# Expert weights of a mixture-of-experts layer: all resident in SBUF and selected by a register on TensorE, instead of one load for each tile

## What is computed

```python
h = patches(x) @ W.T + b                                  # 768 -> 192
h = h + attention(layernorm(h))                           # 12 heads, softmax of scores minus 0.2 x their 8 neighbours
x = layernorm(h)
score = relu(x @ Wr1.T + br1) @ Wr2.T + br2
mask = top_k(score, K); w = softmax(where(mask, score, -inf))
for e in range(E):
    mid = relu(x @ W1[e].T + b1[e]); ye = mid @ W2[e].T + b2[e]
    out = out + w[..., e:e + 1] * ye
h = h + out
```

## Time and profile before

| what | us |
|---|---|
| median of 3 runs | 2078.61 (2074.81 to 2085.45) |
| the profiled execution: span of its instructions | 2041.0 |
| expert phase in it | from 1144.7 |
| first matmul of tile 0 | 1206.69 |
| PE busy | 1849.8 (91% of the span) |
| DVE / ACT / POOL busy | 1458.3 / 1287.1 / 1139.5 |
| `wst` loads | 56 of 1584 KB, median 8.3 to landing |
| HBM read / written | 223.20 MB / 125.83 MB |

### The profile page before, as it was taken

How to read it: one execution, slowest core, us unless ns; L and a number is a source line. 1 busy time by engine, 2 the same in 40 slices (tenths; PEclk the granted TensorE clock), 3 DMA queues, 4 the chain that set the end, 5 groups by cost and what they waited for, 6 DMA issues and landing times. The chain is left out here.

```text
span 2041.0 us, 54475 instructions
## 1 busy us (share of the span) xinstructions
PE 1849.8 (91%) x18013; PEld 1378.2 (68%) x18013; DVE 1458.3 (71%) x4506; ACT 1287.1 (63%) x2661; POOL 1139.5 (56%) x1070
## 2 busy tenths in 40 slices
PE   4898998899889989898898579999999999999996
PEld 4666766666666666666665457777777777767774
DVE  4798889888988898889887456565665655574442
ACT  4688888888888888888888334444444444433332
POOL 4345464645555555555552356766767667664444
PEclk8898999999999999999998569999999999999998
DMA  4586665656566565656554358887888889878985
GB/s 154 147 253 195 186 203 166 196 181 192 174 191 189 179 185 180 194 185 192 174 173 120 102 175 194 197 211 192 199 216 195 198 206 197 198 188 182 187 183 83
DMA packets 362520, 373.10 MB, mean 183 GB/s; under 512 B 144516, under 2 KB 326080, under 8 KB 358272
## 3 DMA queue, kind: packets, MB, share of 16 engines
q1 hardware_dynamic: 320704, 329.03, 55.3%
q0 software_dynamic: 41664, 42.12, 12.3%
HBM read 223.20 MB, written 125.83 MB: 171 GB/s over the span
## 5 line engine op out<-in xcount | busy, mean ns | idle before, releaser
L2021 ACT ACTIVATE mh<-mid_bank 128x512 bf16<-128x512 f32 x336 | 200.6, 597 | 415.2 <-PE mid_bank L1622 415.2
L1923 DVE SCALAR_TENSOR_TENSOR ml<-mid_bank,mh 128x512 bf16<-128x512 f32 x336 | 232.0, 690 | 320.0 <-ACT mh L2021 319.3
L874 DVE TENSOR_REDUCE row_max<-s_bank 98x2 f32<-98x392 f32 x768 | 394.2, 554 | 53.6 <-PE s_bank L650 51.6
L1072 ACT ACTIVATE probs<-t_bank 98x392 f32<-98x392 f32 x768 | 339.7, 499 | 103.9 <-PE t_bank L666 100.5
L2097 POOL DMA_INDIRECT out_rows<-y_out,tail x168 | 267.4, 1592 | 160.7 <-DVE y_out L1957 114.1
L1636 PE MATMUL y_bank<-wst,mh 128*128 128x192 bf16 x1344 | 330.7, 246 | 0.8 <-DVE y_out L1957 0.8
L1639 PE MATMUL y_bank<-wst,ml 128*128 128x192 bf16 x1344 | 330.7, 246 | 0.0
L1638 PE MATMUL y_bank<-wst,mh 128*128 128x192 bf16 x1344 | 330.5, 246 | 0.0
L650 PE MATMUL s_bank<-k_stack,q_stack 96*98 96x196 f16 x1536 | 234.6, 259 | 46.2 <-DVE row_max L874 32.9
L1248 POOL TENSOR_TENSOR x_lo<-x_buf,x_hi 128x588 f16<-128x588 f32 x128 | 170.5, 1344 | 175.1 <-DVE x_b L939 73.0
L666 PE MATMUL t_bank<-q_stack,k_stack 104*98 104x196 f16 x1536 | 225.3, 259 | 32.8 <-ACT probs L1072 29.6
(11 more groups left out here) (257 smaller groups left out, 4527.6 us busy)
## 6 DMA issues: line engine op xcount, KB each, us to landing
wst<-packed SPq DMA_DIRECT2D x56, 1584.0 KB, 8.3
x_buf<-in_x_t SPq DMA_DIRECT2D x32, 1176.0 KB, 7.9
q_stack<-stack_parts SPq DMA_DIRECT2D x288, 98.0 KB, 2.5
k_stack<-stack_parts SPq DMA_DIRECT2D x288, 98.0 KB, 2.6
stack_parts<-qk_hi SPq DMA_DIRECT2D x32, 588.0 KB, 2.9
stack_parts<-qk_lo SPq DMA_DIRECT2D x32, 588.0 KB, 3.1
out_rows<-h_buf SPq DMA_DIRECT2D x32, 294.0 KB
h_in<-out_rows SPq DMA_DIRECT2D x32, 294.0 KB
```

The source lines that it names most:

```text
L874: nc.vector.reduce_max(row_max[st.odd][:, :, hh:hh + 1], s_bank[hh % 2][0:HALF, :, 0:TOKENS], AX.X).then_inc(max_ready, 1)
L1072: nc.scalar.activation(probs[st.odd][:, hh], t_bank[hh % 2][0:HALF, :, 0:TOKENS], ACT.Exp).then_inc(probs_ready, 1)
L1923: nc.vector.scalar_tensor_tensor(ml[n % MID][:], mid_bank[n % MID_PS][:], 0.0, mh[n % MID][:], ALU.max, ALU.subtract).then_inc(ml_ready, 1)
L2021: nc.scalar.activation(mh[n % MID][:], mid_bank[n % MID_PS][:], ACT.Relu).then_inc(mh_ready, 1)
```

## The change

One SBUF tensor `weights` of 2 x 8 x `PACK` columns holds the packed weights of all experts in place of the three buffers `wst`. ACT issues 8 loads of 1584 KB into it at the start of the expert phase, ahead of its first work there. PE waits once, before tile 0, until all have landed. SP no longer reads `expert_i` nor loads weights; it still reads the base. PE reads the expert's number into a register once per tile (`find_expert`), for tile 0 before the main loop and for the others after `hidden` of the last chunk of the tile before. All weight operands, the stationary one in `hidden`, the moving one in `project` and in the biases, are addressed by that register.

The constants `BANK`, `CH`, `TSTEPS`, `SHIFT`, `OFFSET`, `LAST`, `REST_AT` and the functions `groups_for`, `y_bank_of`, `y_at` generalize the loops for other tile sizes. With `T` = 512 they evaluate to 512, 1, 6, 9, 60, 66, 50, and `SELECT`, `DEEP`, and the tile-to-group order come out as before (8, 3, tile i after group i + 7). Buffers and matmuls are the same in number, size and order. A few steps change places within a chunk: DVE computes `tile_gates` one chunk later, in chunk 5 instead of 4; ACT's and DVE's `evict` and ACT's `copy_edge` come ahead of the router's step of the same chunk instead of behind; SP loads the tiles from number 42 on in a loop of their own behind the main one.

The diff, cut to its core; of `project` only the new lines are shown:

```diff
 TJ = T // P
+BANK = 512
+CH = BANK // T
+TSTEPS = FCH // CH
+SHIFT = 9
...
-        wst = [sb(f"wst{i}", [P, 2, PACK], BF16) for i in range(DEEP)]
+        weights = sb("weights", [P, 2 * EXPERTS, PACK], BF16)
...
-        w_in = [sem(f"w_in{i}") for i in range(DEEP)]
+        w_in = sem("w_in")
...
-                e = sp.value_load(expert_i[0:1, i:i + 1], min_val=0, max_val=EXPERTS - 1)
                 at = sp.value_load(base_i[0:1, i:i + 1], min_val=0, max_val=EXPERTS * CAP - T)
-                wait(sp, used, FCH * (i - DEEP + 1))
+                wait(sp, used, TSTEPS * (i - DEEP + 1))
                 wait(sp, xe_ready, i - DEEP + 1)
-                sp.dma_start(wst[q][:], packed.rearrange("(e t) p n -> e t p n", t=2)[bass.ds(e, 1)]
-                             .rearrange("o t p n -> p (o t) n")).then_inc(w_in[q], 16)
                 if i == 0:
-                    for g in range(SELECT - 1):
+                    for g in range(SELECT):
                         sp.wait_ge(sent[g], SENT)
-                last = i + SELECT - 1
-                if last < FGROUPS:
-                    sp.wait_ge(sent[last % RING], SENT * (last // RING + 1))
+                elif i < FULL and groups_for(i) > groups_for(i - 1):
+                    g = groups_for(i) - 1
+                    sp.wait_ge(sent[g % RING], SENT * (g // RING + 1))
                 sp.dma_start_transpose(xT[q][:].bitcast(U16), slots[bass.ds(at, T), 0:XROW]).then_inc(xT_in[q], 16)
...
+            def find_expert(i):
+
+                if tile_there(i):
+                    if i < FULL:
+                        pe.wait_ge(selected, PICK * (i + 1))
+                    else:
+                        pe.wait_ge(plan, TILES_KNOWN)
+                    expert[i] = pe.value_load(expert_i[0:1, i:i + 1], min_val=0, max_val=EXPERTS - 1)
+
+            def part(i, t):
+                return weights[:].rearrange("p (e t) n -> p e t n", t=2)[:, bass.ds(expert[i], 1), t, :].rearrange(
+                    "p o n -> p (o n)")
+
             def hidden(n):
-                i, c = n // FCH, n % FCH
+                i = n // TSTEPS
                 q = i % DEEP
-                if c == 0:
-                    pe.wait_ge(w_in[q], 16 * (i // DEEP + 1))
+                if n % TSTEPS == 0:
+                    if i == 0:
+                        pe.wait_ge(w_in, 16 * EXPERTS)
                     pe.wait_ge(xT_in[q], 16 * (i // DEEP + 1))
                 wait(pe, ml_ready, n - MID_PS + 1)
-                o = mid_bank[n % MID_PS][:]
-
-                def w(b, k=P):
-                    at = b * PART + (c % PCHUNKS) * P
-                    return wst[q][0:k, c // PCHUNKS, at:at + P].bitcast(F16)
-                nc.tensor.matmul(o, w(0), xT[q][:, 0, :], start=True, stop=False)
-                nc.tensor.matmul(o, w(1), xT[q][:, 1, :], start=False, stop=False)
-                nc.tensor.matmul(o, w(2), xT[q][:, 2, :], start=False, stop=False)
-                nc.tensor.matmul(o, w(3), xT[q][:, 0, :], start=False, stop=False)
-                if c == 0:
-                    pe.wait_ge(xe_ready, i + 1)
-                nc.tensor.matmul(o, w(4, HI + 3), xe[q][:], start=False, stop=True).then_inc(mid_ready, 1)
+                for k in range(CH):
+                    c = n % TSTEPS * CH + k
+                    o = mid_bank[n % MID_PS][:, k * T:(k + 1) * T]
+
+                    def w(b, rows=P):
+                        at = b * PART + (c % PCHUNKS) * P
+                        return part(i, c // PCHUNKS)[0:rows, at:at + P].bitcast(F16)
+                    nc.tensor.matmul(o, w(0), xT[q][:, 0, :], start=True, stop=False)
+                    nc.tensor.matmul(o, w(1), xT[q][:, 1, :], start=False, stop=False)
+                    nc.tensor.matmul(o, w(2), xT[q][:, 2, :], start=False, stop=False)
+                    nc.tensor.matmul(o, w(3), xT[q][:, 0, :], start=False, stop=False)
+                    if c == 0:
+                        pe.wait_ge(xe_ready, i + 1)
+                    last = nc.tensor.matmul(o, w(4, HI + 3), xe[q][:], start=False, stop=True)
+                last.then_inc(mid_ready, 1)
 
             def project(n):
...
+                i = n // TSTEPS
                 pe.wait_ge(ml_ready, n + 1)
+                if n % TSTEPS == 0:
+                    wait(pe, evicted, TJ * (i - CH + 1))
+                for k in range(CH):
+                    c = n % TSTEPS * CH + k
+                    at = W1_COLS + (c % PCHUNKS) * DIM
+                    high = part(i, c // PCHUNKS)[:, at:at + DIM]
+                    low = part(i, c // PCHUNKS)[:, W2_COLS + at:W2_COLS + at + DIM]
+                    for j in range(TJ):
+                        cols = slice(k * T + j * P, k * T + (j + 1) * P)
+                        o = y_at(i, j)
+                        nc.tensor.matmul(o, mh[n % MID][:, cols], high, start=(c == 0 and j % 2 == 0), stop=False,
+                                         skip_group_check=True)
+                        nc.tensor.matmul(o, mh[n % MID][:, cols], low, start=False, stop=False, skip_group_check=True)
+                        last = nc.tensor.matmul(o, ml[n % MID][:, cols], high, start=False, stop=False,
+                                                skip_group_check=True)
                 if c == FCH - 1:
+                    biases = weights[:].rearrange("p (e t) n -> p e t n", t=2)[:, bass.ds(expert[i], 1), :,
+                                                                              PACK - BIAS_COLS:]
                     for j in range(TJ):
+                        last = nc.tensor.matmul(y_at(i, j), three[:], biases.rearrange("p o t n -> p (o t) n"),
+                                                start=False, stop=True, skip_group_check=True)
                 last.then_inc(used, 1)
...
             pe.wait_ge(consts_set, CONSTS)
-            for it in range(COMPUTE, ITERATIONS + 1):
+            find_expert(0)
+            for it in range(COMPUTE, LAST + 1):
                 for c in range(FCH):
-                    n = FCH * (it - COMPUTE) + c
-                    if 0 <= n < FCH * NT:
+                    n = FCH * it + c - OFFSET
+                    if 0 <= n < TSTEPS * NT:
                         hidden(n)
...
+                    if n >= 0 and (n + 1) % TSTEPS == 0:
+                        find_expert((n + 1) // TSTEPS)
+                    if 0 <= n - LAG < TSTEPS * NT:
                         project(n - LAG)
...
+            for e in range(EXPERTS):
+                act.dma_start(weights[:, 2 * e:2 * e + 2, :], packed[2 * e:2 * e + 2].rearrange("t p n -> p t n")
+                              ).then_inc(w_in, 16)
             take_xt(0)
```

More of the change, by code:

```diff
@@ L1540, in _ @@
                 load_rows(g)
-            for it in range(ITERATIONS):
+            loaded = 0
+            for it in range(LAST):
                 load_rows(it + AHEAD)
-                if tile_there(it - SELECT):
-                    load_tile(it - SELECT)
+                while loaded < FULL and groups_for(loaded) == it:
+                    load_tile(loaded)
+                    loaded += 1
+            for i in range(FULL, NT):
+                load_tile(i)
             sp.wait_ge(added, 16 * TJ * NT)
@@ L1602, in list_others @@
                     last.then_inc(spares_ready, 1)
+            expert = {}
+            def find_expert(i):
[8 more added lines that the diff above has]
+                    "p o n -> p (o n)")
@@ L2038, in _ @@
             act.wait_ge(consts_set, CONSTS)
-            copy_edge(0)
-            for it in range(COMPUTE, ITERATIONS + 1):
-                i = it - COMPUTE
+            for i in range(CH):
+                copy_edge(i)
+            for it in range(COMPUTE, LAST + 1):
                 for c in range(FCH):
+                    n = FCH * it + c - OFFSET
+                    i = n // TSTEPS
                     if tile_there(i):
-                        take_high_mid(FCH * i + c)
+                        take_high_mid(n)
+                    if n % TSTEPS == 1 and tile_there(i - 1):
+                        evict(i - 1)
+                    if n >= 0 and n % TSTEPS == TSTEPS - 1:
+                        copy_edge(i + CH)
                     if c == 0:
```

113 lines of the change are left out of this document (53 added, 60 removed).

## The result

The changed kernel takes 2089.76 us (median of 20 runs, 2082.2 to 2095.36), the kernel before 2080.98 (20 runs, 2070.72 to 2086.73). The ratio is 1.0038, 95% interval 1.0026 to 1.0050: slower by 0.4%, some 8 us. The forecast was 2077.0, 0.1% faster. The profiled execution of after has a span of 2081.8 us, its own time was 2083.56: 1.8 us lie around the span, not 37.6. So the profiled execution of before that all my rows come from, span 2041.0, was no ordinary one. A *period* is the time from one tile's bias matmuls to the next tile's; a *router tile* has router work beside it, the others have none.

The account below looks back on a forecast made before the run. The prediction took PE's matmul time to bound the steady stretch, with loads and dispatch hidden. From a 2041.0 us span, +2.8 at startup and −4.4 at the tail gave 2039.4, plus 37.6 around it 2077.0 us; range 2066 to 2120.

Parts of the forecast that it names:

- The base: Whole kernel: profiled span 2041.0 us, with the 37.6 us up to the median 2078.61 taken to lie around the span.
- Loads and SP: Steady stretch: removing 56 hidden weight loads and SP's reading and issuing gains 0, since PE never waits for them.
- Register-addressed matmuls: PE's sequencer: 106 a tile at about 0.01 us each, 1.1 us, hidden, so 0.
- Rival B: PE bound by its sequencer: each register-addressed matmul takes 0.1 us instead of 0.01, +107 us, 2184; chance 0.17.
- Address operations: PE's sequencer: 43 addresses a tile at 0.1 us, 4.3 us, hidden because the sequencer runs ahead, so 0.
- Reading the number: PE's sequencer between two chunks: some 0.7 us once a tile, covered by its lead over the matmuls.
- Rival C: Reading the expert's number empties PE's queue, 0.7 us a tile, 39 us less the lead, about 2114; chance 0.10.
- Start: Start of the expert phase: eight weight loads delay the first row load, +2.8 us, bounds 0 and +16.
- Rival D: Warm-up: the weights crowd it at its upper bound, +16 us, 2091; chance 0.08.
- End: After the last tile: POOL's last adds start earlier without weight loads, −4.4 us, bounds −5 and 0.
- Sum: Whole kernel: 2041.0 + 2.8 − 4.4 = 2039.4 us of span, plus 37.6 gives 2077.0 us.
- Rival E: Warm-up's end gains some 5 to 7 us from the missing load, tail −4.4, startup 0, about 2067; chance 0.10.

Follow-up runs that it names:

- after: The changed kernel itself, all expert weights loaded on chip and register-addressed, against the kernel before: 2089.76 us, ratio 1.0038.
- e0: The kernel before, run and profiled once more with no edit: 2077.44 us, span 2073.2 us, ratio 1.0000.
- e1: The changed kernel with expert 0 addressed by constants for every tile, no number read and no register in a matmul: 2077.12 us, ratio 1.0006.
- e2: The changed kernel with the expert's number read once, for tile 0, and that register used for all tiles: ratio 1.0007.
- e4: The changed kernel with the number read once and its register copied afresh each tile, so addresses are formed anew: ratio 1.0040.
- e8: The changed kernel with weight loads spread over the warm-up and two one-column matmuls a tile forming two addresses ahead of the eviction wait: ratio 0.9994.
- e5: The kernel before with PE also reading the expert's number once a tile, the value unused: ratio 1.0019.
- e6: The changed kernel with the expert's number read twice in a row for each tile after the first: ratio 1.0055.
- trace on record: The first profiled execution of the unchanged kernel before, from which the prediction took its rows: span 2041.0 us.
- e3: The changed kernel with the eight weight loads issued one per router group of the warm-up instead of all at once: ratio 0.9988.
- e10: The kernel before with DVE's half of the eviction put ahead of its taking of mid in chunk 1: 2061.35 us, ratio 0.9926.
- e9: The kernel before with POOL's row sends put ahead of the adds of the tile before: 2217.06 us, ratio 1.0667.

## Why the prediction was wrong

- **The base.** "That difference lies around the span": this step was wrong. Of the 37.6 us between that span and the median 1.8 lie outside the span, going by the changed kernel's profile and e0; the execution was a short one, with 15.13 instead of 15.48 in 39 router tiles (13 us), 62.0 instead of 74.7 us to tile 0, and a barrier 7.7 us earlier. An execution outside the range of the runs, 2041 where they began at 2074.81, was to be taken as a warning. The forecast itself doesn't suffer from it, since it adds −1.6 us to the median. But the trace hid that PE waits for the eviction in router tiles: from 1212 to 2019 it has this wait once, for 0.8 us, and e0 has it 29 times from 1300 to 1800 alone.
- **Loads and SP, 0.** Right. The load of 1584 KB per tile was hidden: with and without it a tile takes 15.48 or 15.49 and 12.78 or 12.77 (e0, e1).
- **Register-addressed matmuls, 0.** Right (e2), and so was the count: 43 addresses a tile, 0.12 us apart where I had taken 0.10. Rival B, that each such matmul costs the sequencer 0.1 us, is out. The page of the Trainium skill, "TensorE: Matmul & The Clock Gate", section "Wait — 56ns, not 53.3ns?", gives about 62 ns a matmul when hardware decode is off; no run here shows it for register-addressed ones.
- **Address operations, 0.** Wrong: this is the term that failed. "The sequencer runs ahead and stays hidden, so the term is 0": I compared sums over a tile, 6.7 of 12.78 us, and a sum says nothing about the order. In a tile without router work an operation stands between the wait that comes last and its matmul and is paid in full: 0.16 (e4), of which e8 gives back 0.11. In a usual router tile it is 0.19 (e4 against e2), and PE's idle time lies mostly inside the bias group, by a way that stays open. 39 × 0.19 + 17 × 0.16 = 10.1 us, forecast 0.
- **Reading the number, covered.** Right in tiles without router work (e5) and beside the address operations (e6: twice costs no more); alone in a router tile 0.14. Rival C, 0.7 us in each tile, is out.
- **Start, +2.8, bounds 0 and +16.** Against the trace on record +14.1, against e0 +1.4. That the size came near is luck. "Issuing 8 × 0.39 us ... hidden" failed: the last two issues took 4.18 us each, the first rows came 9.9 us behind the barrier for 2.8, and the first send 7.6 us later than in e0, where 2.8 were forecast. The relief at tile 0, left out of the sum, took back 4.8 of it. "The warm-up goes at the pace of POOL's sends" is not so in the usual executions either: POOL waits for `spot` 27.4 us in 5 waits in e0 (12.3 in one in the trace on record) and 34.1 in 7 in after. Rival D named the crowding, and e3 shows it: 6 us of start.
- **End, −4.4.** Against the trace on record −4.2 (15.4 for 19.6), as forecast; the last tile's adds follow each other at once from 2067.99, 1.0 us after the eviction began at 2066.97. Against e0 −2.5, since e0's end is shorter.
- **Sum.** Forecast −1.6. Measured +8.8 in the medians; in the two spans, +8.6, the periods have +10.6, the start +1.4 and the end −2.5. Rival E's relief at the start is in the changed kernel, but shows only with e3's spread loads (69.8 us to tile 0 for 74.7). The time lay in the range (2066 to 2120), for it held the rivals, but the sign was wrong: no rival had the way by which the 10 us were lost.

## What to carry over

Here an address operation on TensorE's sequencer was free where the sequencer was ahead, and was paid in full behind a wait that came last (0.16 us a tile). So form such addresses before the wait, or make the wait early. Loads that are hidden in the steady stretch bring nothing there when they are removed, and putting them all at the start costs (here 6 us): issue them one by one beside the first work. Before a trace is used as a base, hold its execution's time against the other runs; one that lies outside them may lack the very wait that matters.

## What the runs showed of the hardware

- A register in a matmul's operand, moving or stationary, cost TensorE nothing: a tile has 106, and takes 12.77 us with registers (e2) and with constants (e1). Forming an address took 46 ns, and 0.12 us from one to the next (after).
- Issuing loads in a row can hold the engine that issues them: with eight loads of 1584 KB the seventh and eighth took 4.18 us to issue, the others 0.43 to 0.92 (after; 4.2 to 4.5 in e1, e2, e4 and e6). Spread out, they took 0.37 to 0.43 each (e3).
- In e0 ACT took up the result of a hidden layer 1.7 us late once per router tile, at the end of POOL's row sends: the matmul's semaphore change was recorded 1.7 us after its end, where 0.01 is usual. With another order of DVE's work (e10) it was 0.7 us late and cost nothing; with the sends ahead of the adds (e9) such stretches stand behind the adds. In after PE itself stops in this stretch. Its cause is open.
